# Mixing stage split in two: all tiles normalised and turned first, the recurrence's steps placed between the rest's matmuls

## The reference, cut to what matters

```python
xn = _layernorm(x); x_ = (xn normalised again) * ln_w + ln_b
u  = x_ @ Ws.T + bs + x_ @ Wi.T + bi                    # 16 states a row
h  = jnp.tanh(h @ A.T + u_t)                            # for each of 2048 rows in turn
s  = (H @ Wo.T + bo) * sigmoid(x_ @ Wg.T + bg) + xn
k  = jax.nn.relu((xn @ Win + bin_)[..., None] * W1 + b1)
g  = _silu((einsum(k, W2) + b2) @ Wout + bout)
x  = x + s * g
# layer 1: attention over 4 batches, 8 experts with top-2 routing; the change leaves it as it is
```

## Time and profile before

| | |
|---|---|
| median of 3 runs | 1534.09 us (1532.28 to 1534.9) |
| the profiled execution | 1534.16 us, its span 1532.4 us |
| PE busy | 1275.9 us, 83% of the span |
| DVE busy | 1047.1 us, 68% |
| POOL busy, ACT busy | 674.1 us (44%), 583.1 us (38%) |
| mean granted TensorE clock | 0.91 |

### The profile page before, as it was taken

How to read it: one execution, slowest core, us unless ns; L and a number is a source line. 1 busy time by engine, 2 the same in 40 slices (tenths; PEclk the granted TensorE clock), 3 DMA queues, 4 the chain that set the end, 5 groups by cost and what they waited for, 6 DMA issues and landing times. The chain is left out here.

```text
span 1532.4 us, 23065 instructions
## 1 busy us (share of the span) xinstructions
PE 1275.9 (83%) x7727; PEld 878.4 (57%) x7727; DVE 1047.1 (68%) x1889; ACT 583.1 (38%) x851; POOL 674.1 (44%) x540
## 2 busy tenths in 40 slices
PE   2999997759888999424999999999999999999800
PEld 1665554438777777413567657667667765766600
DVE  2787773046999999878666756666666665676547
ACT  0555553212222222100535544553544454464322
POOL 2112220003666666612245453454455544555459
PEclk9999998659999999755999999999999999999955
DMA  9000003200000000011325343342433434343367
GB/s 306 1 0 0 0 0 160 114 14 28 28 28 28 29 29 29 15 55 28 89 47 113 44 84 72 44 111 46 94 62 63 98 42 102 57 80 69 48 192 260
DMA packets 82186, 103.90 MB, mean 68 GB/s; under 512 B 14352, under 2 KB 73616, under 8 KB 80688
## 3 DMA queue, kind: packets, MB, share of 16 engines
q0 software_dynamic: 25008, 35.31, 14.6%
q1 hardware_dynamic: 42144, 59.80, 11.5%
q10 hardware_dynamic: 14944, 7.62, 1.7%
HBM read 58.40 MB, written 44.30 MB: 67 GB/s over the span
## 5 line engine op out<-in xcount | busy, mean ns | idle before, releaser
L1593 ACT ACTIVATE e_h_all<-e_pH,e_b1c,e_h_scale 128x512 f32<-128x512 f32 x256 | 199.6, 780 | 297.7 <-PE e_pH L1641 296.5
L1398 POOL DMA_INDIRECT expert_sums<-e_yo,e_dcol x128 | 211.1, 1650 | 178.2 <-DVE e_yo L1550 148.9
L1660 PE MATMUL e_pY<-e_w_hi,e_h_hi 128*128 128x256 f16 x1024 | 279.3, 273 | 4.8 <-DVE e_w_lo L1474 4.8
L1661 PE MATMUL e_pY<-e_w_lo,e_h_hi 128*128 128x256 f16 x1024 | 279.1, 273 | 0.0
L1662 PE MATMUL e_pY<-e_w_hi,e_h_lo 128*128 128x256 f16 x1024 | 279.1, 273 | 0.0
L1384 POOL DMA_INDIRECT e_xg<-xn_rows,e_icol x136 | 158.1, 1163 | 197.2 <-DVE e_icol L1415 155.5
L1515 DVE TENSOR_TENSOR e_h_lo<-e_h_all,e_h_hi 128x512 f16<-128x512 f32 x256 | 176.9, 691 | 62.4 <-ACT e_h_hi L1593 56.9
L1639 PE MATMUL e_pH<-e_x_hi,e_w_hi 128*128 128x512 f16 x512 | 197.0, 385 | 11.1 <-issue 8.5
L1641 PE MATMUL e_pH<-e_x_hi,e_w_lo 128*128 128x512 f16 x512 | 197.2, 385 | 0.0
L1640 PE MATMUL e_pH<-e_x_lo,e_w_hi 128*128 128x512 f16 x512 | 197.0, 385 | 0.0
L1073 PE MATMUL c_pY<-late,c_xnT 128*128 128x256 f32 x512 | 130.0, 412 | 0.0
(11 more groups left out here) (227 smaller groups left out, 2327.5 us busy)
## 6 DMA issues: line engine op xcount, KB each, us to landing
raw<-expert_w SPq DMA_DIRECT2D x18, 1024.0 KB, 5.5
expert_sums<-r_zero SPq DMA_DIRECT2D x10, 1024.0 KB, 13.1
xn_rows<-c_xn SPq DMA_DIRECT2D x16, 512.0 KB, 3.0
f_ya<-expert_sums SPq DMA_DIRECT2D x16, 512.0 KB, 5.5
out<-f_ya SPq DMA_DIRECT2D x16, 512.0 KB, 3.8
x_st<-x ACTq DMA_DIRECT2D x4, 1536.0 KB, 13.9
e_xg<-xn_rows,e_icol POOLq DMA_INDIRECT x136, 3.0
x_st<-x SPq DMA_DIRECT2D x4, 512.0 KB, 9.1
```

The lines of the kernel that those rows point to most:

```text
L1398: pool.indirect_dma_start(v.y_dram, bass.IndirectOffsetOnAxis(dcol[u][:, q:q + 1], axis=0), yo[u][:, q, :], None, bounds_check=N + CAP - 1 ...
L1593: last = act.activation(dst, pH[h % NPH][:, :], ACT.Relu, bias=b1c[eu][:, h:h + 1], scale=h_scale[eu][:, 0:1])
L1660: pe.matmul(pY[:, q, :], h_hi[:, h, cols], w2_hi[:, h, :], start=(h == 0), stop=False)
L1661: pe.matmul(pY[:, q, :], h_hi[:, h, cols], w2_lo[:, h, :], start=False, stop=False)
```

## The change

1. `prepare`: the input's remaining twelve DMAs (tiles 4 to 15) move from ACT's queue, where four large ones waited for the first tiles to land, to SP's queue behind the first four, each of 512 KB, with one semaphore per four tiles. The late weights now come behind them on SP's queue.
2. `mix`, part one: for all 16 tiles DVE measures, POOL makes the powers for two tiles at a time, the tile is normalised (one of four batches on DVE, three on ACT), PE turns it, ACT copies it into `prod_st`, where it stays until its gate is written there, PE makes the recurrence's input, DVE takes it. SP's zeroing of `expert_sums` (from a 128x256 tile of zeros read eight times) starts once all tiles are turned.
3. `mix`, part two: DVE normalises each tile a second time, since `finish` needs it, and G, K, S, Z run as before. At four places of a tile (`step`, slots 0 to 3) PE and ACT run one step of the recurrence: two matmuls (`u_st` by the identity, then `at_blk`) and a tanh. 48 steps fill tiles 0 to 11. The loops are written out.
4. `recur` keeps only the test of the flag and the extra sweeps.

```diff
             def _(sp):
...
+                for n in range(1, NT // FIRST):
+                    for b in range(B):
+                        rows = v.x[b, n * FIRST * P:(n + 1) * FIRST * P, :]
+                        sp.dma_start(v.x_st[:, n * FIRST:(n + 1) * FIRST, b * D:(b + 1) * D],
+                                     rows.rearrange("(t p) d -> p t d", p=P)).then_inc(v.x_in[n - 1], 16)
...
-                act.wait_ge(v.x_first, 16 * B)
-                for b in range(B):
-                    act.dma_start(v.x_st[:, FIRST:, b * D:(b + 1) * D],
-                                  v.x[b, FIRST * P:, :].rearrange("(t p) d -> p t d", p=P)).then_inc(v.x_in, 16)
...
             def _(dve):
...
+                def first_rows(t):
+                    dve.wait_ge(r_ready, t // PAIR + 1)
+                    if t >= 2:
+                        dve.wait_ge(t_done, t - 1)
+                    dve.tensor_scalar(xn[t % 2][:, 0, :], v.x_st[:, t, 0:D], mv[:, t, 0, 0:1], r1[:, t, 0:1],
+                                      ALU.subtract, ALU.mult).then_inc(first_xn, 1)
...
+                for t in range(PAIR):
+                    measure(t)
+                for t in range(NT):
+                    if t + PAIR < NT:
+                        measure(t + PAIR)
+                    first_rows(t)
+                    if t:
+                        take_u(t - 1)
+                take_u(NT - 1)
...
             def _(act):
...
+                for t in range(NT):
+                    rows(t)
+                    if t:
+                        take_turned(t - 1)
+                take_turned(NT - 1)
...
             def _(pe):
...
+                for t in range(NT):
+                    turn(t)
+                    if t:
+                        recurrence_input(t - 1)
+                recurrence_input(NT - 1)
...
+                def step(t, slot):
+                    for j, n, l in steps_at(t, slot):
+                        if j:
+                            pe.wait_ge(state, j)
+                        ins = pe.matmul(pR[j % 2], ident, v.u_st[:, l, :], start=True, stop=(j == 0),
+                                        skip_group_check=True)
+                        if l:
+                            ins = pe.matmul(pR[j % 2], v.at_blk, v.h_st[:, l - 1, :], start=False, stop=True,
+                                            skip_group_check=True)
```

More of the change, by code:

```diff
@@ L386, in mix @@
         sf = sb("a_sf", [P, B * D])
[L387 to L393, removed]
+        st = [sb(f"a_st{n}", [P, B, 6]) for n in range(2)]
+        mv = sb("a_mv", [P, NT, B, 2])
+        r1 = sb("a_r1", [P, NT, B])
+        nmr = sb("a_nmr", [P, NT, B])
+        again = sb("a_again", [P, NT, B])
+        ta = sb("a_ta", [P, PAIR, B])
+        tb = sb("a_tb", [P, PAIR, B])
+        mhalf = sb("a_mhalf", [P, PAIR, B])
+        mone = sb("a_mone", [P, PAIR, B])
+        eps = sb("a_eps", [P, PAIR, B])
+        zero = sb("a_zero", [P, D])
+        ends = sb("r_ends", [P, NCH])
+        diff = sb("r_diff", [P, NCH])
+        differs = sb("r_differs", [P, 1])
         pT = psum("a_pT", [P, KD, BANK])
@@ L488, in finish @@
[L488 to L498, removed]
@@ new lines, in _ @@
+                for t in range(NT):
+                    step(t, 0)
+                    act.wait_ge(y_ready, t + 1)
+                    act.activation(v.prod_st[:, t, :], v.prod_st[:, t, :], ACT.Tanh, scale=0.5).then_inc(thy_ready, 1)
+                    act.wait_ge(kan_done, t + 1)
+                    act.activation(gT[:, :], pGU[:, :], ACT.Identity, bias=v.gconst[:, 0:1]).then_inc(gT_ready, 1)
+                    step(t, 1)
+                    if t + 1 < NT:
+                        take_s(t + 1)
+                    step(t, 2)
+                    if t + 1 < NT:
+                        units(t + 1)
+                    act.wait_ge(z_done, t + 1)
+                    if t:
+                        act.wait_ge(p_done, t)
@@ new lines, in _, with inner, step @@
+                recurrence_input(NT - 1)
+                def inner(t):
+                    for k in range(KD):
+                        last = pe.matmul(pS[:, :], v.win2[:, k, :], xnT(t)[:, k, :], start=(k == 0), stop=(k == KD - 1))
+                    last.then_inc(s_done, 1)
+                def step(t, slot):
+                    for j, n, l in steps_at(t, slot):
+                        if j:
[5 more added lines that the diff above has]
+                                            skip_group_check=True)
+                        elif n:
+                            ins = pe.matmul(pR[j % 2][:, 1:NCH], v.at_blk, v.h_st[:, L - 1, 0:NCH - 1],
+                                            start=False, stop=True, skip_group_check=True)
+                        ins.then_inc(summed, 1)
@@ L602, in body @@
+                pe.wait_ge(u_evac, NT)
+                pe.wait_ge(v.late_in, 32)
+                inner(0)
+                for t in range(NT):
+                    if t:
+                        pe.wait_ge(y_ready, t)
                     for b in range(B):
                         for k in range(KD):
-                            last = pe.matmul(pG[:, b, :], xnT[:, k, b * P:(b + 1) * P], v.wgate[:, k, :],
+                            last = pe.matmul(pG[:, b, :], xnT(t)[:, k, b * P:(b + 1) * P], v.wgate[:, k, :],
@@ L614, in body @@
                     last.then_inc(kan_done, 1)
[L615 to L617 removed]
+                    step(t, 1)
+                    if t + 1 < NT:
+                        inner(t + 1)
+                    step(t, 2)
+                    if t:
+                        pe.wait_ge(sf_ready, t)
                     for n in range(2):
@@ L626, in body @@
                     last.then_inc(z_done, 1)
-                pairs(pe, body)
+                    step(t, 3)
+                    if t == NT - 2:
+                        pe.wait_ge(compared, 2)
+                        pe.matmul(pT[0:1, 0, 0:1], differs[:, :], v.ones[:, 0:1], start=True, stop=True).then_inc(counted, 1)
 def recur(nc, v):
     with ExitStack() as c:
-        sem = v.sem
-        ends = c.enter_context(nc.sbuf_tensor("r_ends", [P, NCH], F32))
-        diff = c.enter_context(nc.sbuf_tensor("r_diff", [P, NCH], F32))
@@ L684, in sweep @@
                                   start=False, stop=True, skip_group_check=True).then_inc(summed, 1)
-                sweep(0, first=True)
-                for n in range(1, SWEEPS):
-                    sweep(n)
-                pe.wait_ge(compared, 2)
-                pe.matmul(pf[0:1, 0:1], differs[:, :], v.ones[:, 0:1], start=True, stop=True).then_inc(counted, 1)
                 pe.wait_ge(flagged, 1)
-                again = pe.value_load(flag[0:1, 0:1], min_val=0, max_val=P)
+                again = pe.value_load(v.flag[0:1, 0:1], min_val=0, max_val=P)
                 with pe.If(again > 0):
```

318 lines of the change are left out of this document (160 added, 158 removed).

## The result

The changed kernel takes 1538.12 us (median of nine runs, 1535.53 to 1539.82), the kernel before took 1534.09 us beside it (nine runs, 1531.08 to 1535.92): a ratio of 1.0027 [1.0017, 1.0037]. It is 4 us slower, just over the 3 us that a measurement can tell here; 17 were forecast. The profiled execution took 1538.11 us, its span is 1536.3 us.

What follows compares the result with a forecast made beforehand. PE was taken to bound the mixing, latency the recurrence. Start -4.5, recurrence -70.4 + 2.0, turns and inputs -26.6, steps +24, part one +101.1 less 8.0, waits and rounding 0.7: 16.9 us later, 1551.0 us; range 1524 to 1562.

Steps and rivals of the forecast that it cites:

- part one's ring: Part one, each tile: DVE, PE, PE, DVE run one after the other, 6.4 us at PE's slow clock.
- S(0): Part two's first S, after thin PE work: at the slow clock, 3.6 us.
- The sign: Whole kernel: slower 0.77, faster by over 0.2% 0.20, within 0.2% 0.03.
- The start: Before the mixing: SP issues 16 DMAs at 1.07 us each, mixing starts at 21.3, 4.5 us sooner.
- A step: Recurrence step on PE in part two: four passes of 128 columns, 0.5 us, between 0.43 and 0.98.
- The tile without them: Part two, a tile without turn, input and steps: 13.12 - 0.93 - 0.79 = 11.40 us.
- The end: From attend's start on: the same list of instructions on every engine, time taken as before.
- dear step: Rival, part two: both matmuls of a step pay wait and load anew, 0.98 a step, +23, 1574 us; 8%.
- late state: Rival, part two: ACT over 1.4 us late to step 3, PE stalls; 1 us over gives +12, 1563 us; 4%.
- a clock that is up for part of the time: Case for PE's clock in part one: kernel within 0.2% of before; 0.03.
- likeliest case: Part one's ring as forecast: 1551 us, its own range 1537 to 1561; 70%.
- The rival at full clock: Part one with PE at full clock: ring 4.94 us, part one 78.3 instead of 101.1, kernel 1526 us; 18%.

Runs made afterwards that it cites:

- e2_start: Changed kernel with SP issuing only tiles 0 to 7 in prepare, the rest inside the mixing's block; 1522.5 us, 0.9925 of the kernel before.
- e7_actq: Changed kernel with the input of tiles 4 to 15 issued from ACT's queue again, in four large DMAs; 1536.42 us in a single run.
- e4_warm: Changed kernel plus ten bf16 matmuls with unused result behind each tile's recurrence input in part one; 1523.01 us, 0.9926 of the kernel before.
- e5_double: Changed kernel with the first matmul of each of the 48 steps in part two issued twice; 1546.17 us, 1.0082 of the kernel before.
- e1_ring: Changed kernel with DVE taking the recurrence's input two tiles behind instead of one in part one; 1494.03 us, 0.9746 of the kernel before.
- e6_nosteps: Changed kernel with the 48 steps moved out of part two, back into the recur block; 1578.8 us, 1.0313 of the kernel before.

## Why the prediction was right in mechanism and wrong in size

Right is the mechanism: the change hides the recurrence and pays for it with a ring. The ring stands in the profile link by link, with DVE's forecast wait of 3.5 us before L514 (3.53), and PE in part two never waits for ACT's states (197.10 of 197.10 us). Wrong is the size: `attend` was forecast 16.9 us later than before and started 6.15 us later, at 327.44 instead of 338.2. The steps that failed are the prices of part one's ring (6.4 us, measured 5.95), 5.0 us too much in all, and of part two's tiles (13.4 and 11.40 us, measured 12.87 and 11.18), 7.0 too much; the gain of 4.5 at the start failed the other way, by 5.3. Term by term:

| step of the prediction | forecast | measured | off by |
|---|---|---|---|
| mixing starts | 21.3 | 26.56 | +5.3 |
| part one, to `first_rows(2)` | 15.75 | 14.4 | -1.3 |
| eleven rings | 11 x 6.4 = 70.4 | 11 x 5.95 = 65.4 | -5.0 |
| part one's rest | 14.95 | 14.5 | -0.5 |
| S(0) | 3.6 | 1.8 | -1.8 |
| twelve tiles with steps | 13.4 each | 12.87 each | -6.3 |
| three tiles without | 11.40 each | 11.18 each | -0.7 |
| the last G and K | 7.4 | 7.2 | -0.2 |
| last Z to `attend` | 9.8 | 9.5 | -0.3 |
| from `attend` to the end | as before | 2.2 less | -2.2 |

They make the 13 us between 1551 and 1538.

*The sign* owes something to luck. Had the start come at 21.3 as forecast and all else as measured, the kernel would have been 1.3 us faster than before, which can't be told from no change. The 4 us of loss are there because an error of 5.3 us at the start stood against 18 us of terms that were too dear.

*The start* is wrong in its reasoning: "four take 4.27 us, so 1.07 us each". The first four issues are not the pace of a long list. The twelve behind them take 18.24 / 12 = 1.52 us each, as long as 512 KB take to land: the window from 5.5 to 23.7 shows 352 GB/s, and the first 25 us of the kernel before 335. `e2_start` and `e7_actq` fit this: the same 18.23 us wherever the barrier stands, and nearly the same end on ACT's queue. The forecast gain of 4.5 us was a loss of 0.7.

*The ring's size.* The ring at half clock is 6.17 us, not 6.4. `measure` takes 106.41 - 104.70 = 1.71 us and not 1.95, which was read where DVE's rows had small gaps between them; the turn's slot is 0.25 longer than forecast (102.57 - 100.67 = 1.90), and the hop behind the last matmul about 0.2 shorter. The same holds at full clock: 4.65 in `e4_warm` where 4.94 was forecast. The other 0.22 us down to 5.95 is the clock, which I had at 0.50 throughout from 30 to 120 us; six of the eleven rings are shorter than 6.17, with a part of the turn or of the input at full clock. In the runs that leave part one's order alone its length was 90.6 to 94.7 us, by how often the clock rose. The argument for the slow clock had left out a stretch of the same recurrence at full clock, though PE was busy for only half of it (a line of the trace before, columns as in the earlier trace rows):

```profile
257.00:262.60 5.60, 2.85 (x13) 1.73 (x12) 0.00 (x0) 2.20 (x6) 0.00 (x0) 0.99 1.00 413
```

*S(0)* came behind two inputs and a turn in close succession, and the clock had risen by then.

*A step* was taken at 0.5 and costs 0.445 (12.89 - 11.11 = 1.78 for four), four dense passes, which `e5_double` confirms. *The tile without them* was taken as 13.12 less the slots of turn and input, 1.72; from one G to the next (288.27 to 299.38) it takes 11.11, 2.01 shorter. Most of the other 0.29 is a wait of PE that the prediction put at nothing ("no PE row in it waits"). The waits of before, from 60 to 230 us, show it in ten tiles of thirteen, and in the tile that was read the turn also starts (230.21) as DVE's `normalise` ends (228.77 + 1.38 = 230.15):

```profile
PE a_pT L579 <- DVE a_xn L484: 2.4, 10, 0.2
```

With the turn gone the wait is gone: K's slot fell from 230.21 - 226.43 = 3.78 to 3.58 us. G's fell from 3.65 to 3.55, now that no narrow matmuls stand before it. The first tile takes 12.66 us (its step 0 lacks a matmul) and the last but one 11.32 (the flag's matmul stands in it), so the means of the table are 12.87 and 11.18.

*The end.* Everything behind `attend`'s start was taken as unchanged. Its list is, but its time differs by 3 us between the profiles, and the 2.2 us here have no shown cause.

*The rivals.* Neither a dear step nor a late state came. The clock in part one was neither 0.50 nor 1.00 but moved between them; this case, "a clock that is up for part of the time", had been given 3%. The 1538 us lie inside the likeliest case's own 1537 to 1561, at its very edge. The rival at full clock named 78.3 us for part one, where `e4_warm` had 80.2; the two are close by luck in part, for its rings were 3.2 us shorter in all than forecast and its idle matmuls cost some 4.

What stays open: what raises and lowers the clock. The profile shows 1.00 with PE busy for 31.29 of 52.6 us in `e1_ring`, and 0.66 and 0.77 with 50.38 of 94.4 and 44.49 of 77.9. No run varied that alone.

## What to carry to other kernels

Moving a chain of latencies under the bound engine's work pays as hoped (here 41 to 47 us of 70), but look at what the stage that is left behind looks like: a producer and a consumer that are asked for the same tile's result in the same round run one after the other, and one round of distance in one list (`take_u(t - 2)`) was worth 44 us. Read a stage's clock from the durations of its matmuls, not from the mean of a window in which PE also waits. And look at the waits view of the whole stage before calling an engine unbroken: a wait of 0.2 us in each tile doesn't show in every timeline. Look, too, at what stands ahead of a barrier: issues that only feed later tiles held the changed kernel up for 13 us.

## What the runs showed of the hardware that was not expected

- DMA issues on one queue: the first 4 x 512 KB in 4.23 us, then twelve in 18.24 us, 1.52 each, the rate at which they land (352 GB/s in that window). SP's engine is blocked meanwhile, and with it a barrier behind it.
- A stage can gain by useless PE work: 34 us of dummy matmuls in part one made it 14 us shorter, since the clock went from 0.66 to 1.00.
- Sixteen transposes alone, after 23 us without work, were followed by the full clock: 417 ns each at first, the last 273 (changed kernel; `e6_nosteps` the same).
- The granted clock of a window read 1.00 from 34.9 to 36.9 us, in which each transpose took 417 ns as in windows of 0.50. It was the first work after a long idle stretch, and only the durations told.
- A step of two matmuls of 128 columns in fp32 costs PE 0.445 us between dense groups, and each further pair of passes 0.22.
- POOL's power of eight values a partition takes 1.64 us where four take 1.01, and three ACT rows of 128x256 with scale and bias from memory take 1.57 us together.
